# A blocked triangular solve that keeps its probabilities unscaled and puts the row's reciprocal into the row step

## The chip, the cores and the metric

The kernel runs on one core of a Trainium2 chip. The metric is the device time of one execution in microseconds (us). Engines are named as in the profile: PE (matrix engine; PEld is its weight load), DVE (vector engine), ACT (scalar engine), POOL (GpSimd) and SP (the queue that issues most DMAs).

## What is computed

Two layers on an input of 8 x 512 x 128 floats. The change lies in the attention of the second layer; its last lines decide:

```python
probs = jax.nn.softmax(logits + causal_mask, axis=-1)
L = jnp.eye(s) - jnp.tril(probs, -1)
rhs = jnp.diagonal(probs, axis1=-2, axis2=-1)[..., None] * v
A = jax.scipy.linalg.solve_triangular(L, rhs, lower=True)
return A.transpose(0, 2, 1, 3).reshape(b, s, HID) @ Wd.T + bd
```

For each of 8 x 16 = 128 pairs of batch and head, with head width 8 and 512 positions, row t of A is `p[t,t] * v[t]` plus the sum over all earlier rows k of `p[t,k] * A[k]`. Here p is a softmax: an exponential E divided by the row's sum Z.

## The kernel before

The 128 pairs of batch and head lie on the 128 partitions. The 512 positions are taken in four blocks I of 128. For each block `attend` makes the exponentials (tile `Ed` holds those of the block's own square), and sums up, over all keys of earlier blocks, `E * A` and the row sum Z; both lie in `RT`. Then `solve_block` solves the block itself, in four quarters c of 32 positions. The feed-forward experts of the layer (`ExpertSteps`, 10 tiles in each block, 2, 2, 3 and 3 of them in the four quarters) run in the same stretch on PE, ACT and POOL.

One quarter of `solve_block` goes as follows.

- PE turns the quarter's exponentials (`turn_probs`, L1179, 16 transposes for half a quarter) into a bank. DVE multiplies them out of the bank by `rZ = 1/Z` into `Pn` (L1293). They are then probabilities.
- DVE turns what earlier blocks add (`turn_before`, L1285), takes the reciprocal (L1286), multiplies the sums by `rZ` into `term` (L1279) and adds that to `A` (L1282, in `add_term`).
- POOL multiplies `A` (so far v) by the diagonal of `Pn` (L1263) and then sets the diagonal to 1 (L1266).
- From the second quarter on, DVE also copies the rows of the quarter before, turned by PE (`turn_rows`, L1218), into `Apos` (`keep_rows`, L1301; ACT copies the other half at L1254). PE makes 128 small products of them with `Ed` (`later_sums`, L1228; each stands in the trace as two matmuls, 256 in all); DVE turns the result (L1305), multiplies by `rZ` and adds it (`add_later`).
- DVE runs the row steps: for r = 1 to 31, two multiplies (L1323, four of the eight head columns each, 4(r+1) elements) and two sums over k (L1329). Every step waits for the step before by the semaphore `row_done`: 124 instructions in a quarter.

Queues around it, in program order. PE, in quarter c: turns of quarter c+1, the expert tiles of quarter c, `turn_rows(c)`, `later_sums(c+1)`. ACT: for each expert tile a copy (L775), two GELUs (L782) and a copy (L789), then its half of the rows (L1254). POOL: L1263, L1266, then for each expert tile a copy of indices (L796) and two scattered DMAs (L800). DVE has no work of the experts here.

Of the kernel before, what the change touches and what calls it, by code (L numbers as in the profile page):

```python
# [12 lines left out]
P = 128  # L13
# [7 lines left out]
HD = D // NH  # L21
BH = B * NH
CAP = 1280
SUB = 32
# [893 lines left out]
def solve_attention(nc, A, Apos, Ed, rows_dram, o_dram, send_rest, w, k_stack, q_stack, vT_dram, max_dram):  # L918
# [10 lines left out]
    with ExitStack() as ctx:  # L929
# [15 lines left out]
        rZ = sb("rZ", [P, P])  # L945
        before = sb("before", [P, SUB, SUB])
        prod = sb("prod", [P, HD, SUB])
        later, term = sb("later", [P, SUB, SUB]), sb("later_term", [P, SUB, HD])
        mx = sb("mx", [P, 2, BH])
        mxp = sb("mxp", [P, 3, BH], BF16)  # L950
        mxT = sb("mxT", [P, 3, P], BF16)
# [23 lines left out]
        for I in range(-1, LT):  # L975
            attend(nc, I, A, vT_dram, ident, Kst, Qmax, Qexp, k_stack, q_stack, max_dram, mx, mxp, mxT,
                   masks, identb, Ed, Eoff, Apos, one, RT, bank, big, send_rest)
            if I >= 0:
                solve_block(nc, I, Ed, RT, before, rZ, Pn, prod, later, term, A, Apos, ident, bank, big[3], steps)


def attend(nc, I, A, vT_dram, ident, Kst, Qmax, Qexp, k_stack, q_stack, max_dram, mx, mxp, mxT, masks,
# [197 lines left out]
    return last  # L1180


def solve_block(nc, I, Ed, RT, before, rZ, Pn, prod, later, term, A, Apos, ident, bank, wide, steps):

    k0 = I * steps.N // LT
    tiles = [range(k0 + sum(TILES[:c]), k0 + sum(TILES[:c + 1])) for c in range(NSUB)]
# [3 lines left out]
    with ExitStack() as ctx:  # L1190
# [16 lines left out]
        @block.tensor  # L1207
        def _(pe):
            def turn_next(c):
                for g in range(per_sub * c, per_sub * (c + 1)):  # L1210
                    if g >= 2:
                        pe.wait_ge(probs_in, g - 1)
                    turn_probs(nc, Ed, ident, bank[g % 2], g).then_inc(probs_turned, 1)

            def turn_rows(c):
                pe.wait_ge(row_done, ops * (c + 1))
                for d in range(HD):
                    last = nc.tensor.transpose(wide[0:(c + 1) * SUB, d * P:(d + 1) * P], A[:, d, t0:t0 + (c + 1) * SUB], ident[:, :])  # L1218
                    if d % 4 == 3:
                        last.then_inc(rows_turned, 1)  # L1220

            def later_sums(c):
                pe.wait_ge(act_kept, c)
                pe.wait_ge(dve_kept, c)
                for t in range(SUB):
                    for g in range(4):
                        row = (I * BH + 4 * t + g) * (HD + 1)
                        last = nc.tensor.matmul(wide[SUB * g:SUB * (g + 1), t * SUB:(t + 1) * SUB], Apos[0:c * SUB, row:row + SUB],  # L1228
                                                Ed[0:c * SUB, SUB * g + t, c * SUB:(c + 1) * SUB], start=True, stop=True,
                                                skip_group_check=True)  # L1230
                last.then_inc(later_mm, 1)

            turn_probs(nc, Ed, ident, bank[1], 1).then_inc(probs_turned, 1)
            for c in range(NSUB):
                if c + 1 < NSUB:
                    turn_next(c + 1)
                for k in tiles[c]:
                    steps.turn(pe, k)
                    steps.up(pe, k)
                    steps.down(pe, k)  # L1240
                turn_rows(c)
                if c + 1 < NSUB:
                    later_sums(c + 1)

        @block.scalar
        def _(act):
            for c in range(NSUB):
                for k in tiles[c]:
                    steps.keep_turned(act, k)
                    steps.gelu(act, k)  # L1250
                    steps.keep_out(act, k)
# [3 lines left out]

        @block.gpsimd
        def _(pool):
            for c in range(NSUB):
                ts = slice(t0 + c * SUB, t0 + (c + 1) * SUB)
                first = c * SUB * SUB  # L1260
                diag = Pn.rearrange("p q k -> p (q k)")[:, first:first + (SUB - 1) * (SUB + 1) + 1:SUB + 1]
# [2 lines left out]
                                        ALU.mult).then_inc(own_done, 1)  # L1264
                pool.wait_ge(own_done, 2 * c + 1)
                nc.gpsimd.memset(diag, 1.0).then_inc(own_done, 1)  # L1266
                for k in tiles[c]:
                    steps.send(pool, k)
            if I == LT - 1:
# [3 lines left out]
        def _(dve):  # L1273
            base = Chain(dve, base_done)

            def add_term(c, sums):
                qs = slice(c * SUB, (c + 1) * SUB)
                ts = slice(t0 + c * SUB, t0 + (c + 1) * SUB)
                base(nc.vector.tensor_tensor(term[:, :, :], sums[:, :, 0:HD],  # L1279
                                             rZ[:, qs].rearrange("p (q a) -> p q a", a=1).broadcast_to([P, SUB, HD]), ALU.mult))  # L1280
                dve.wait_ge(own_done, 2 * c + 1)
                base(nc.vector.tensor_tensor(A[:, :, ts], A[:, :, ts], term[:, :, :].rearrange("p q d -> p d q"), ALU.add))  # L1282

            def turn_before(c):
                base(nc.vector.transpose(before[:, :, :], RT[:, c, :, :].rearrange("p t q -> p q t")))  # L1285
                base(nc.vector.reciprocal(rZ[:, c * SUB:(c + 1) * SUB], before[:, :, HD]))  # L1286

            def add_before(c):
                for g in range(per_sub * c, per_sub * (c + 1)):
                    gs = slice(g * TURN, (g + 1) * TURN)  # L1290
                    if g:
                        dve.wait_ge(probs_turned, g)
                    nc.vector.tensor_tensor(Pn[:, gs, :], bank[g % 2][:, 0:TURN * SUB].rearrange("p (q k) -> p q k", k=SUB),  # L1293
                                            rZ[:, gs].rearrange("p (q a) -> p q a", a=1).broadcast_to([P, TURN, SUB]),
                                            ALU.mult).then_inc(probs_in, 1)
                add_term(c, before)

            def keep_rows(c):
                ks = slice(c * SUB, (c + 1) * SUB)
# [2 lines left out]

            def add_later(c):
                dve.wait_ge(later_mm, c)
                base(nc.vector.transpose(later[:, :, :], wide[:, :].rearrange("p (t q) -> p q t", q=SUB)))  # L1305
                add_term(c, later)

            for c in range(NSUB):
                turn_before(c)
                if c:  # L1310
                    keep_rows(c - 1)
                add_before(c)
                if c:
                    add_later(c)
                dve.wait_ge(own_done, 2 * c + 2)
                k0 = t0 + c * SUB
                for r in range(1, SUB):
                    n = ops * c + 4 * (r - 1)
                    for i in range(2):
                        if r > 1:  # L1320
                            dve.wait_ge(row_done, n - 1 + i)
                        ds = slice(i * HD // 2, (i + 1) * HD // 2)
                        nc.vector.tensor_tensor(prod[:, ds, 0:r + 1], A[:, ds, k0:k0 + r + 1],  # L1323
                                                Pn[:, c * SUB + r:c * SUB + r + 1, 0:r + 1].broadcast_to([P, HD // 2, r + 1]),
                                                ALU.mult).then_inc(row_done, 1)
                    for i in range(2):
                        dve.wait_ge(row_done, n + 1 + i)
                        ds = slice(i * HD // 2, (i + 1) * HD // 2)
                        nc.vector.tensor_reduce(A[:, ds, k0 + r], prod[:, ds, 0:r + 1], AX_X, ALU.add).then_inc(row_done, 1)  # L1329
            keep_rows(NSUB - 1)  # L1330


# [308 lines left out]
```

## Time and profile before

| | us |
|---|---|
| median of 3 runs | 1409.95 (1408.22 to 1410.42) |
| the profiled execution | 1409.06 |
| its span, first to last instruction | 1407.1 |
| PE busy in it | 979.8 (70%) |
| DVE busy | 910.4 (65%) |
| ACT busy | 466.4 (33%) |
| POOL busy | 342.9 (24%) |
| mean granted TensorE clock | 0.821 |

The profile is of one execution, and all rows below are of that one. "x992" is a count; in the list of groups the number behind the bar is busy time in us, then the mean length of one instruction in ns, then idle time of the engine before such instructions and who ended it. In a timeline each row is one instruction, or a run of like ones without idle time between them: start, length of the run, engine, line, operation, tiles, count, and in brackets the idle time before it with who ended it. A granted clock of 1.00 is 2.4 GHz, 0.50 is 1.2 GHz. "issue" means that the engine waited for nothing that the profile shows.

### The profile page before, as it was taken

The numbers are of one execution on the slowest core, as the hardware profiler recorded it, in microseconds if no ns is written. First come the engines' busy times: TensorE is split into PE (matmuls) and PEld (weight loads), VectorE is DVE, ScalarE is ACT, GpSimd is POOL, SyncE is SP. The second block draws the span as 40 slices with busy tenths as digits, with TensorE's granted clock in tenths as the row PEclk, the third lists the DMA queues.
The fourth block names the chain that finished last, engine by engine and source line by source line (L and its number), as shares of the span: only waits on it lengthen the run. The fifth ranks groups of instructions, "written<-read, shape, count | busy, mean of one in ns | idle before, by whom it ended". The sixth has DMA issues, their size and how long they took to land. (4 is left out here: it accounts for less than half of the span.)

```text
span 1407.1 us, 29569 instructions
## 1 busy us (share of the span) xinstructions
PE 979.8 (70%) x10741; PEld 766.5 (54%) x10762; DVE 910.4 (65%) x3559; ACT 466.4 (33%) x1066; POOL 342.9 (24%) x390
## 2 busy tenths in 40 slices
PE   5376599970665057876769967769986768986754
PEld 5265499960621034665646556646665656765643
DVE  5666272216789065788858889858878970068767
ACT  1233244424224003311235411235522227931115
POOL 1277155540047170021210021210001220012221
PEclk9998799995579587966889966889977888986777
DMA  9397598836018864410044220044411005420008
GB/s 225 40 212 206 145 250 241 230 96 179 25 50 238 244 149 123 111 28 18 25 97 129 73 61 20 21 110 126 116 44 32 26 22 163 137 57 23 25 22 234
DMA packets 241824, 153.95 MB, mean 109 GB/s; under 512 B 80432, under 2 KB 226096, under 8 KB 241424
## 3 DMA queue, kind: packets, MB, share of 16 engines
q1 hardware_dynamic: 232528, 133.04, 37.1%
q0 software_dynamic: 9152, 19.02, 4.1%
q8 instruction: 86, 1.41, 0.4%
q14 instruction: 58, 0.48, 0.1%
HBM read 96.76 MB, written 55.24 MB: 108 GB/s over the span
## 5 line engine op out<-in xcount | busy, mean ns | idle before, releaser
L1157 DVE TENSOR_REDUCE mx<-banks 128x1 f32<-128x384 f32 (+3 forms) x352 | 203.1, 635 | 74.0 <-PE banks L1088 58.9
L1323 DVE TENSOR_TENSOR prod<-A,Kst_Pn 128x8 f32<-128x8 f32 (+30 forms) x992 | 179.5, 221 | 0.5
L1329 DVE TENSOR_REDUCE A<-prod 128x4 f32<-128x8 f32 (+30 forms) x992 | 174.8, 217 | 0.0
L800 POOL DMA_INDIRECT o_dram<-step_o,step_to x80 | 81.9, 1024 | 308.5 <-ACT step_o L789 296.3
L1137 ACT ACTIVATE Eoff<-banks 128x256 f32<-128x256 f32 (+2 forms) x192 | 114.9, 599 | 102.6 <-PE banks L1073 93.5
L1071 PE MATMUL banks<-Qexp,Kst_Pn 128*128 128x256 bf16 x640 | 115.4, 282 | 47.5 <-DMA Qmax<-q_stack 37.8
L1139 ACT ACTIVATE Ed<-banks 128x256 f32<-128x256 f32 x256 | 97.9, 382 | 111.5 <-PE banks L1073 111.5
L1084 PE MATMUL banks<-masks,identb 128*128 128x128 bf16 (+2 forms) x352 | 89.2, 254 | 61.0 <-DMA Qmax<-q_stack 51.1
L756 PE MATMUL banks<-step_xT,step_w 128*128 128x256 f32 x320 | 106.3, 490 | 22.5 <-issue 22.0
L1263 POOL TENSOR_TENSOR A<-A,Kst_Pn 128x256 f32<-128x256 f32 x16 | 15.8, 987 | 411.6 <-DVE Kst_Pn L1293 411.6
L1088 PE MATMUL banks<-Kst_Pn,Qmax 128*128 128x128 bf16 (+3 forms) x491 | 115.7, 306 | 0.0
L767 PE MATMUL banks<-step_w,step_h 128*128 128x128 f32 x640 | 94.1, 307 | 28.3 <-ACT step_h L782 28.3
L767 PEld LDWEIGHTS banks<-step_w,step_h 128*128 128x128 f32 x640 | 85.8, 216 | 48.7 <-ACT step_h L782 48.7
L1071 PEld LDWEIGHTS banks<-Qexp,Kst_Pn 128*128 128x128 bf16 x640 | 56.3, 100 | 84.0 <-DMA Qmax<-q_stack 38.9
L756 PEld LDWEIGHTS banks<-step_xT,step_w 128*128 128x128 f32 x320 | 74.7, 245 | 46.1 <-issue 33.8
L596 POOL DMA_INDIRECT o_dram<-e_o,e_to x78 | 76.2, 977 | 92.7 <-DVE e_o L617 80.5
L1179 PE MATMUL banks<-ident_c,Ed 32*128 32x32 f32 x512 | 78.5, 325 | 16.3 <-PEq L83 10.4
L587 ACT ACTIVATE e_h<-banks,e_b 128x256 f32<-128x256 f32 x156 | 63.2, 471 | 80.0 <-PE banks L557 80.0
L1179 PEld LDWEIGHTS banks<-ident_c,Ed 32*128 32x128 f32 x512 | 75.9, 254 | 19.0 <-issue 13.1
L1160 DVE COPY RT<-banks 128x512 f32<-128x512 f32 x32 | 22.1, 691 | 90.9 <-PE banks L1102 90.9
L557 PE MATMUL banks<-e_xT,e_w 128*128 128x256 f32 x312 | 76.2, 388 | 5.7 <-DMA e_b<-in_L_ffn_b_dram 5.0
L1084 PEld LDWEIGHTS banks<-masks,identb 128*128 128x128 bf16 x352 | 35.2, 100 | 80.6 <-DMA Qmax<-q_stack 52.9
(197 smaller groups left out, 1832.5 us busy)
## 6 DMA issues: line engine op xcount, KB each, us to landing
Kst_Pn<-k_stack SPq DMA_DIRECT2D x32, 512.0 KB, 4.1
rows_dram<-blank SPq DMA_DIRECT2D x12, 858.0 KB, 11.6
e_w<-in_L_w1T_dram SPq DMA_DIRECT2D x39, 256.0 KB
e_w<-in_L_w2T_dram SPq DMA_DIRECT2D x39, 256.0 KB
Qmax<-q_stack SPq DMA_DIRECT2D x64, 96.0 KB
Qexp<-q_stack SPq DMA_DIRECT2D x64, 96.0 KB
Kst_Pn<-k_stack SPq DMA_DIRECT2D x16, 384.0 KB, 4.3
step_xt<-rows_dram SPq DMA_DIRECT2D x40, 132.0 KB, 2.2
```

The costliest lines, as they stand in the source:

```text
L756: last = self.nc.tensor.matmul(self.up_banks[i][:, (hc % 2) * TS:(hc % 2 + 1) * TS], self.w1[e % 2][:, hc * P:(hc + 1) * P], self.xT[:, :] ...
L767: last = self.nc.tensor.matmul(self.down_bank[:, j * D:(j + 1) * D], self.h[:, hc, j * P:(j + 1) * P], self.w2[e % 2][:, hc, :], start=(hc ...
L800: self.nc.gpsimd.indirect_dma_start(self.o_dram, bass.IndirectOffsetOnAxis(self.to[n][:, j:j + 1], 0), self.o[n][:, j, :], None).then_inc( ...
L1071: last = nc.tensor.matmul(out, Kst[b % 2][:, s, J * P:(J + 1) * P], Qexp[b % 2][:, 2 * s:2 * s + 2, :], start=True, stop=(J < I), skip_gro ...
L1084: nc.tensor.matmul(diagonal, identb[:, :], masks[:, 0:1, :].broadcast_to([P, per_bank, P]), start=True, stop=False, skip_group_check=True)
L1088: last = nc.tensor.matmul(out[:, j * keys_ahead:(j + 1) * keys_ahead], Qmax[b % 2][:, h, :], Kst[b % 2][:, h // 2, 0:keys_ahead], start=Fa ...
L1137: nc.scalar.activation(Eoff[:, n % 4, 0:I, :, :].rearrange("p j h q -> p (j h q)"), big[n % n_big][:, 0:I * 2 * P], ACT.Exp, scale=scale)
L1139: nc.scalar.activation(Ed[:, :, :].rearrange("p (g t) q -> p g t q", g=4)[:, 2 * (n % 2):2 * (n % 2) + 2, n // 2, :], big[n % n_big][:, I ...
L1157: nc.vector.tensor_reduce(out, logits, AX_X, ALU.max, negate=True).then_inc(max_done, 1)
L1179: last = nc.tensor.transpose(out[:, i * SUB:(i + 1) * SUB], Ed[ks, :, g * TURN + i], ident[ks, ks])
L1323: nc.vector.tensor_tensor(prod[:, ds, 0:r + 1], A[:, ds, k0:k0 + r + 1], Pn[:, c * SUB + r:c * SUB + r + 1, 0:r + 1].broadcast_to([P, HD / ...
L1329: nc.vector.tensor_reduce(A[:, ds, k0 + r], prod[:, ds, 0:r + 1], AX_X, ALU.add).then_inc(row_done, 1)
```

## The change

- `Pn` holds exponentials that aren't divided by Z. ACT copies them out of the bank (`keep_probs`), where DVE multiplied them; for quarter c+1 it does so ahead of the expert tiles of quarter c.
- The sums of earlier blocks and of earlier quarters are added to `A` unscaled, straight from the turned tile; the multiplies by `rZ` into `term` are gone.
- The division is done in the row step: the two multiplies become `scalar_tensor_tensor` with `rZ[:, row]`, one value for each partition, as the scalar. Row 0 of a quarter, which had no step, gets one multiply of 128x8.
- In `later_sums` the two sides are exchanged: `Ed` is loaded as weights and 8 columns of `Apos` stream, where 32 columns of `Apos` were the weights and 32 of `Ed` streamed. The result takes 256 columns of the bank and not 1024, so DVE turns 128x256.
- POOL's `own(c+1)` (L1263, L1266) goes ahead of the sends of quarter c. DVE turns what earlier blocks add to quarter c+1 right behind `keep_rows(c-1)`, and in the first quarter ahead of the row steps; the reciprocal and the add stand ahead of `keep_rows`.

```diff
             def turn_rows(c):
-                pe.wait_ge(row_done, ops * (c + 1))
+                pe.wait_ge(row_done, (ops + 1) * (c + 1))
...
-                        last = nc.tensor.matmul(wide[SUB * g:SUB * (g + 1), t * SUB:(t + 1) * SUB], Apos[0:c * SUB, row:row + SUB],
-                                                Ed[0:c * SUB, SUB * g + t, c * SUB:(c + 1) * SUB], start=True, stop=True,
-                                                skip_group_check=True)
+                        last = nc.tensor.matmul(wide[SUB * g:SUB * (g + 1), t * HD:(t + 1) * HD],
+                                                Ed[0:c * SUB, SUB * g + t, c * SUB:(c + 1) * SUB], Apos[0:c * SUB, row:row + HD],
+                                                start=True, stop=True, skip_group_check=True)
...
         def _(act):
+            def keep_probs(c):
+                for g in range(per_sub * c, per_sub * (c + 1)):
+                    if g:
+                        act.wait_ge(probs_turned, g)
+                    nc.scalar.copy(Pn[:, g * TURN:(g + 1) * TURN, :],
+                                   bank[g % 2][:, 0:TURN * SUB].rearrange("p (q k) -> p q k", k=SUB)).then_inc(probs_in, 1)
+
+            keep_probs(0)
             for c in range(NSUB):
+                if c + 1 < NSUB:
+                    keep_probs(c + 1)
                 for k in tiles[c]:
...
         def _(pool):
-            for c in range(NSUB):
+            def own(c):
...
+            own(0)
+            for c in range(NSUB):
+                if c + 1 < NSUB:
+                    own(c + 1)
                 for k in tiles[c]:
                     steps.send(pool, k)
...
-            def add_term(c, sums):
-                qs = slice(c * SUB, (c + 1) * SUB)
+            def add_sums(c, sums):
                 ts = slice(t0 + c * SUB, t0 + (c + 1) * SUB)
-                base(nc.vector.tensor_tensor(term[:, :, :], sums[:, :, 0:HD],
-                                             rZ[:, qs].rearrange("p (q a) -> p q a", a=1).broadcast_to([P, SUB, HD]), ALU.mult))
-                dve.wait_ge(own_done, 2 * c + 1)
-                base(nc.vector.tensor_tensor(A[:, :, ts], A[:, :, ts], term[:, :, :].rearrange("p q d -> p d q"), ALU.add))
+                base(nc.vector.tensor_tensor(A[:, :, ts], A[:, :, ts], sums, ALU.add))
...
+            def add_before(c):
                 base(nc.vector.reciprocal(rZ[:, c * SUB:(c + 1) * SUB], before[:, :, HD]))
...
+                dve.wait_ge(own_done, 2 * c + 2)
+                add_sums(c, before[:, :, 0:HD].rearrange("p q d -> p d q"))
...
-                base(nc.vector.transpose(later[:, :, :], wide[:, :].rearrange("p (t q) -> p q t", q=SUB)))
-                add_term(c, later)
-
+                base(nc.vector.transpose(later[:, :, :], wide[:, 0:SUB * HD].rearrange("p (t d) -> p d t", d=HD)))
+                add_sums(c, later[:, :, :])
+
+            turn_before(0)
             for c in range(NSUB):
-                turn_before(c)
+                add_before(c)
                 if c:
                     keep_rows(c - 1)
-                add_before(c)
+                if c + 1 < NSUB:
+                    turn_before(c + 1)
                 if c:
                     add_later(c)
-                dve.wait_ge(own_done, 2 * c + 2)
-                k0 = t0 + c * SUB
+                k0, q0 = t0 + c * SUB, c * SUB
+                n = (ops + 1) * c + 1
+                nc.vector.tensor_tensor(A[:, :, k0], A[:, :, k0], rZ[:, q0:q0 + 1].broadcast_to([P, HD]), ALU.mult).then_inc(row_done, 1)
+                dve.wait_ge(row_done, n)
                 for r in range(1, SUB):
-                    n = ops * c + 4 * (r - 1)
                     for i in range(2):
...
-                        nc.vector.tensor_tensor(prod[:, ds, 0:r + 1], A[:, ds, k0:k0 + r + 1],
-                                                Pn[:, c * SUB + r:c * SUB + r + 1, 0:r + 1].broadcast_to([P, HD // 2, r + 1]),
-                                                ALU.mult).then_inc(row_done, 1)
+                        nc.vector.scalar_tensor_tensor(out=prod[:, ds, 0:r + 1], in0=A[:, ds, k0:k0 + r + 1], scalar=rZ[:, q0 + r:q0 + r + 1],
+                                                       in1=Pn[:, q0 + r:q0 + r + 1, 0:r + 1].broadcast_to([P, HD // 2, r + 1]),
+                                                       op0=ALU.mult, op1=ALU.mult).then_inc(row_done, 1)
```

## Rows read from the trace of the kernel before

**Rows 1.** The costliest groups of instructions on the page: the multiplies of the row steps

```profile
L1323 DVE TENSOR_TENSOR prod<-A,Kst_Pn 128x8 f32<-128x8 f32 (+30 forms) x992 | 179.5, 221 | 0.5
```

**Rows 2.** Timeline of DVE: the head of the third block, up to its second row step

```profile
1042.78 2.53 DVE L1285 STREAM_TRANSPOSE before<-RT 128x1024 f32<-128x1024 f32 x1 [2.66 <-PEq L83]
...
1048.26 0.70 DVE L1282 TENSOR_TENSOR A<-A,later_term 128x256 f32<-128x256 f32 x1 [0.91 <-POOL A L1263]
1048.99 0.24 DVE L1323 TENSOR_TENSOR prod<-A,Kst_Pn 128x8 f32<-128x8 f32 x2
...
1049.39 0.25 DVE L1323 TENSOR_TENSOR prod<-A,Kst_Pn 128x12 f32<-128x12 f32 x2
```

**Rows 3.** Timeline of DVE: from the end of quarter 0 to the rows of quarter 1

```profile
1065.74 0.48 DVE L1323 TENSOR_TENSOR prod<-A,Kst_Pn 128x128 f32<-128x128 f32 x2
1066.14 0.47 DVE L1329 TENSOR_REDUCE A<-prod 128x4 f32<-128x128 f32 x2
1066.53 1.94 DVE L1285 STREAM_TRANSPOSE before<-RT 128x1024 f32<-128x1024 f32 x1
...
1068.89 1.04 DVE L1301 COPY Apos<-banks 32x512 f32<-32x512 f32 x1
...
1075.80 1.25 DVE L1305 STREAM_TRANSPOSE later<-banks 128x1024 f32<-128x1024 f32 x1 [2.98 <-PE banks L1228]
...
1077.55 0.69 DVE L1282 TENSOR_TENSOR A<-A,later_term 128x256 f32<-128x256 f32 x1
1078.27 0.24 DVE L1323 TENSOR_TENSOR prod<-A,Kst_Pn 128x8 f32<-128x8 f32 x2
```

**Rows 4.** Timeline of DVE in the first layer: instructions with a scalar per partition, back to back

```profile
325.01 1.14 DVE L669 SCALAR_TENSOR_TENSOR c_r<-c_r,wt 128x128 f32<-128x128 f32 x4 [17.20 <-ACT c_r L691]
327.72 0.88 DVE L669 SCALAR_TENSOR_TENSOR c_r<-c_r,wt 128x128 f32<-128x128 f32 x3 [1.57 <-ACT c_r L691]
...
74.68 1.13 DVE L357 SCALAR_TENSOR_TENSOR s<-banks,rq,xr 128x128 f32<-128x128 f32 x4 [1.95 <-PE banks L272]
```

**Rows 5.** Timeline of POOL: its multiply in the third block, a copy near the end

```profile
1047.11 1.04 POOL L1263 TENSOR_TENSOR A<-A,Kst_Pn 128x256 f32<-128x256 f32 x1 [120.28 <-DVE Kst_Pn L1293]
...
1377.39 0.62 POOL L1372 COPY rows_b<-Apos 128x512 f32<-128x512 f32 x1 [1.77 <-PE banks L1393]
```

**Rows 6.** Timeline of DVE in the stretch of that copy

```profile
1376.90 1.51 DVE L1432 SCALAR_TENSOR_TENSOR last_r<-last_r,wt 128x128 f32<-128x128 f32 x4 [14.24 <-ACT last_r L1412]
```

**Rows 7.** Groups of instructions by line: ACT copies of a bank into SBUF

```profile
L182 ACT COPY xnT<-banks 128x512 f32<-128x512 f32 x8 | 4.7, 587 | 15.7 <-PE banks L165 15.7
```

**Rows 8.** Timeline of PE in the third block: turns, and the small products

```profile
1042.78 2.50 PE L1179 MATMUL banks<-ident_c,Ed 32*128 32x32 f32 x16 [3.13 <-PEq L83]
...
1070.08 1.99 PE L1228 MATMUL banks<-Ed,Apos 32*32 32x32 f32 x130 [2.37 <-DVE Apos L1301]
1073.75 1.93 PE L1228 MATMUL banks<-Ed,Apos 32*32 32x32 f32 x126 [1.69 <-issue]
...
1102.93 1.50 PE L1228 MATMUL banks<-Ed,Apos 64*32 64x32 f32 x94 [1.72 <-issue]
...
1127.75 1.04 PE L1218 MATMUL banks<-ident_c,A 128*96 128x128 f32 x8
1130.10 1.67 PE L1228 MATMUL banks<-Ed,Apos 96*32 96x32 f32 x167 [1.31 <-DVE Apos L1301]
```

**Rows 9.** Windows of PE: stretch, length, busy time (count), granted clock, DMA share, GB/s

```profile
1066.66:1067.70 1.04, 1.04 (x8) 1.00 0.19 63
1070.10:1075.70 5.60, 3.91 (x257) 0.50 0.03 6
1130.10:1135.20 5.10, 2.87 (x257) 0.93 0.11 32
1298.50:1300.41 1.91, 1.91 (x8) 0.50 0.20 69
```

**Rows 10.** Timeline of DVE: the wait at the end of quarter 2

```profile
1128.89 1.05 DVE L1301 COPY Apos<-banks 32x512 f32<-32x512 f32 x1 [2.03 <-PE banks L1218]
```

More of the change, by code:

```diff
@@ L947, in solve_attention @@
         prod = sb("prod", [P, HD, SUB])
-        later, term = sb("later", [P, SUB, SUB]), sb("later_term", [P, SUB, HD])
+        later = sb("later", [P, HD, SUB])
         mx = sb("mx", [P, 2, BH])
@@ L978, in solve_attention @@
             if I >= 0:
-                solve_block(nc, I, Ed, RT, before, rZ, Pn, prod, later, term, A, Apos, ident, bank, big[3], steps)
+                solve_block(nc, I, Ed, RT, before, rZ, Pn, prod, later, A, Apos, ident, bank, big[3], steps)
 def attend(nc, I, A, vT_dram, ident, Kst, Qmax, Qexp, k_stack, q_stack, max_dram, mx, mxp, mxT, masks,
@@ L1180, in turn_probs, with solve_block @@
     return last
-def solve_block(nc, I, Ed, RT, before, rZ, Pn, prod, later, term, A, Apos, ident, bank, wide, steps):
+def solve_block(nc, I, Ed, RT, before, rZ, Pn, prod, later, A, Apos, ident, bank, wide, steps):
     k0 = I * steps.N // LT
@@ L1274, in _ @@
             base = Chain(dve, base_done)
-            def add_term(c, sums):
-                qs = slice(c * SUB, (c + 1) * SUB)
+            def add_sums(c, sums):
                 ts = slice(t0 + c * SUB, t0 + (c + 1) * SUB)
-                base(nc.vector.tensor_tensor(term[:, :, :], sums[:, :, 0:HD],
-                                             rZ[:, qs].rearrange("p (q a) -> p q a", a=1).broadcast_to([P, SUB, HD]), ALU.mult))
-                dve.wait_ge(own_done, 2 * c + 1)
-                base(nc.vector.tensor_tensor(A[:, :, ts], A[:, :, ts], term[:, :, :].rearrange("p q d -> p d q"), ALU.add))
+                base(nc.vector.tensor_tensor(A[:, :, ts], A[:, :, ts], sums, ALU.add))
             def turn_before(c):
                 base(nc.vector.transpose(before[:, :, :], RT[:, c, :, :].rearrange("p t q -> p q t")))
+            def add_before(c):
                 base(nc.vector.reciprocal(rZ[:, c * SUB:(c + 1) * SUB], before[:, :, HD]))
[L1288 to L1296, printed above, removed]
+                dve.wait_ge(own_done, 2 * c + 2)
+                add_sums(c, before[:, :, 0:HD].rearrange("p q d -> p d q"))
             def keep_rows(c):
@@ L1329, in _ @@
                         nc.vector.tensor_reduce(A[:, ds, k0 + r], prod[:, ds, 0:r + 1], AX_X, ALU.add).then_inc(row_done, 1)
+                    n += 4
             keep_rows(NSUB - 1)
```

## Prediction

> **What bounds the kernel now.** I read the page first: the row steps of the solver are among its costliest groups, 992 multiplies with almost no idle time ahead of them [rows 1]. Then I read DVE's timeline through one block. In the third block quarter 0 starts its rows at 1048.99 [rows 2] and ends them at 1066.14 + 0.47 = 1066.61 [rows 3], so the row phase takes 17.62 us, and DVE doesn't pause in it. Sixteen such phases make 282 us of the span. Between two row phases lies a chain over three engines: PE turns the rows, DVE and ACT copy them (DVE from 1068.89), PE makes the small products from 1070.08, DVE waits 2.98 for them, turns, multiplies, adds, and the rows of quarter 1 start at 1078.27 [rows 3, 8]. That is 11.66 us. The reader should see that the multiplies by 1/Z which DVE does meanwhile lie in front of a wait for PE: they are no part of this chain, and taking them away only makes the wait longer. What counts is DVE's row phase, and behind it the chain of turn, copy, products and add. One quarter differs. At the end of quarter 2 DVE waits 2.03 for PE's turned rows [rows 10], and PE had no wait ahead of that turn [rows 8]: three expert tiles hold PE longer than the rows hold DVE. So a slower row phase costs time in quarters 0, 1 and 3 of each block, and in quarter 2 only beyond that wait.
>
> **The change part by part**, for one block; there are four.
>
> *Row steps.* Each quarter has 62 multiplies, and all of them become multiplies with a scalar per partition. The two multiplies of 128 elements in the last row start 0.40 before the sum behind them, 0.20 each [rows 3]. Four `scalar_tensor_tensor` of 128 elements, back to back, take 1.14 together and three take 0.88; that gives 0.26 from start to start [rows 4]. So the scalar costs 0.06 us per instruction, and since these starts follow each other without a wait, nothing hides it. 62 x 0.06 = 3.8 us. In the shortest rows the chain already waits: the first row takes 1049.39 - 1048.99 = 0.40 [rows 2], about 0.07 more than four issues of such length, and some ten rows have a falling part of that; this absorbs about 0.3. I take 3.5 us for a quarter, with 3.0 and 3.8 as ends. An end at nothing, or below, would need the scalar's fetch to lie under the instruction ahead; the rows speak against it, and it is a rival below. On the path it counts three times: +10.5 us.
>
> Here two rules of the Trainium skill can be held against the rows. The page "VectorE: DVE Perf Modes" (section "The TRN2 errata — SBUF-src ops pay a fixed extra latency per instruction") gives a vector instruction from SBUF to SBUF a fixed 58 cycles plus its elements, and names no term for a scalar operand; by that, an estimate from its figures, both kinds of multiply take 0.19 us at 128 elements and the row step costs nothing. Its figure fits the plain multiply (0.20) and not the one with a scalar (0.26), so the measured row decides. The page "Vector Engine (DVE) Microarchitecture Reference" (section 7, "Points that are easy to get wrong") says that a `scalar_tensor_tensor` with two SBUF sources that aren't bf16 runs at half throughput. In this trace it doesn't: four of them with both sources in SBUF take 1.14, and four with one source in PSUM take 1.13 [rows 4].
>
> *Small products.* The count stays, 256 matmuls, and so does the stall in the middle of them, in which PE waits for nothing that the profile shows ("issue", 1.69 and 1.72 here [rows 8]); I take it for a wait for PE's own instructions. At a granted clock of 0.50 130 matmuls take 1.99, 0.0153 each; at 0.93 167 take 1.67, 0.0100 each [rows 8, 9]. With 8 columns to stream and not 32 I take 0.0100 at the low clock too. The part ahead of the stall is bound to the arrival of instructions, so only the 126 behind it gain: 126 x 0.005 = 0.6. At the high clock I count 0.2. For the three rounds of a block: -1.1 us, with 0 and -2.0 as ends.
>
> *From the products to the rows.* Now 1078.27 - (1073.75 + 1.93) = 2.59. After it: a wait of 0.1, a turn of 256 columns in place of 1024 (between 1.25 / 4 = 0.31 and 0.5, I take 0.45), an add of 0.65, row 0's multiply of 0.2 with its wait, and gaps between them: 1.5. This gains 1.05 in quarters 1 and 3: -2.1 us. In quarter 2 it falls into the wait for PE.
>
> *From the rows to the products.* Now DVE's turn and reciprocal stand ahead of its copy, and products start 1070.08 - 1066.61 = 3.47 behind the rows [rows 3, 8]. Afterwards a reciprocal and an add (1.0 us) stand there and PE's turn decides: 1.04 at a granted clock of 1.00, 1.91 at 0.50 [rows 9]. With 0.15 for two semaphores and 1.19 from the copy's start to the products, that gives 2.4 or 3.25. Both levels stand in this trace ahead of like work. PE finishes its tiles first and will then sit idle for the rest of a row phase that is longer than now, so I take the low clock: -0.3 in quarters 0 and 1, -0.6 us in all; at the high clock it is -2.1. At the end of quarter 3 the same turn may come at the low clock too, +0.8; I count half, +0.4.
>
> *The head.* Now 6.21 from the block's start to the first row [rows 2]. After it, ACT's copy of the second half (0.59 [rows 7]) follows PE's 16 turns of 2.50 [rows 8], then POOL's multiply of 1.04 [rows 5] and its memset: DVE gets to its add at about 4.5, adds until 5.3, turns quarter 1's sums for 1.94 ahead of the rows, and does row 0's multiply: 7.4. +1.2 us. The turn moved here was not on the chain in quarter 1 except ahead of the copy, which is counted above.
>
> *POOL's multiply inside the row phase.* Now DVE waits for it between phases. After it, `own(c+1)` runs as soon as ACT has copied, during the rows of quarter c. A POOL copy of 0.62 that reads SBUF stretched four `scalar_tensor_tensor` from 1.14 to 1.51 [rows 4 to 6], 0.37 lost. POOL's multiply takes 0.96 to 1.04, so about 0.6 is lost in each of quarters 0 and 1: +1.2 us (ends 0 and 1.9). In quarter 2 it is covered by the wait for PE.
>
> *ACT's copies.* 8 x 0.59 in a block. The second one of each quarter starts when PE goes on to turn the first tile, and ACT's copy of that tile queues behind it, and PE behind that: between 0 and 0.6, I take 0.45. In quarter 2, where PE decides, that is +0.45 us (the upper end is 2, should PE's clock rise one tile later). Elsewhere it hides under the rows. That quarter has room for the rest: products end at 1102.93 + 1.50 = 1104.43, the copy starts at 1128.89, so PE's way takes 24.46 [rows 8, 10]; DVE's takes 1.5 + 17.62 + 3.5 + 0.6 + 1.0 = 24.2. If that cover were gone, each further 0.1 us would count.
>
> Sum for a block: 10.5 - 1.1 - 2.1 - 0.6 + 0.4 + 1.2 + 1.2 + 0.45 = +9.95. Four blocks: +39.8. The profiled execution took 1409.06 (0.89 under the median of the three runs), so the forecast is 1409.06 + 39.8 = 1449 us. The multiplies that leave DVE (Pn, term) give nothing beyond this, since they lay before waits for POOL or PE.
>
> **The rivals.**
>
> *The chain's shortening is worth more.* PE keeps the high clock at the turns (-2.1 in place of -0.6), the products gain 2.0, the clock costs nothing at the end, POOL's multiply fits between, and a row phase costs 3.2: 9.6 - 2.0 - 2.1 - 2.1 + 1.2 + 0.45 = +5.05 a block, 1429 us. Against it speaks the longer idle time of PE ahead of each turn. 0.14.
>
> *The scalar is free.* This is the side of a gain: if its fetch lies under the instruction ahead, the row phase stays at 17.62, and the shortened chain remains, 1.2 + 1.2 - 1.1 - 2.1 - 0.6 + 0.45 = -0.95 a block, 1405 us; without POOL's collision 1400. It decides once the scalar costs a multiply under 0.95 / (3 x 62) = 0.005 us. For it: these instructions wait on semaphores, those in [rows 4] don't. Against it: these waits are nearly all over by the time of issue in the long rows. Its chance is 0.08. By the cost table of the Trainium skill's page "VectorE: DVE Perf Modes", named above, this rival would hold.
>
> *Two SBUF sources halve the rate.* A multiply streams 0.001 us per element, 68 elements on average, so a quarter would lose 62 x 0.068 = 4.2 more, and quarter 2 would lose its cover: +4.2 x 3 + 4.3 = 17 a block more, 1517 us. The rows show no such thing [rows 4]. 0.02.
>
> *The change doesn't do what it says* in one part: the exchanged products stay bound to the arrival of instructions. That is the end of 0 above, +4.4 us: 1453, inside the forecast.
>
> **How the numbers follow.** The forecast case, 1432 to 1466, has 0.76; with the first rival at 0.14, the free scalar at 0.08 and the halved rate at 0.02. The range of 8 in 10 goes from 1422 to 1466. A difference under 0.2% (2.8 us) can't be told from no change here. Slower by more than that takes the forecast and both slower rivals, 0.92 less 0.03 for what I don't see: 0.89. Faster has 0.08, same 0.03.
>
> **What the profile will show.** Right: the multiplies of the row step about 0.06 longer and a row phase of about 21 us; a turn of 128x256 of about 0.45; DVE's copy behind the rows about 2 us after them; one stretched row step in quarters 0 and 1; quarter 2 unchanged in length from products to copy. The forecast is wrong if the row phase stays under 18.5, if quarter 2 gets longer by more than 1 us, or if the head gets shorter.

## The result and the profile after

| | before | after |
|---|---|---|
| median (us) | 1410.18 (1408.22 to 1412.49) | 1444.14 (1442.37 to 1445.11) |
| ratio after / before | | 1.0232, 95% interval 1.0213 to 1.0251 |
| the profiled execution | 1409.06 | 1443.83 |
| its span | 1407.1 | 1441.8 |

The change makes the kernel 2.3% slower: 34.8 us between the two profiled executions, where +39.8 was forecast. The row steps, in the list of groups of after (columns as in [rows 1]):

```profile
L1331 DVE SCALAR_TENSOR_TENSOR prod<-A,rZ,Kst_Pn 128x8 f32<-128x8 f32 (+30 forms) x992 | 246.2, 289 | 0.6
```

Against [rows 1] the same 992 multiplies are busy 66.7 us longer (246.2 - 179.5). The timeline of DVE in the third block of after shows the head and the first row steps (these answer to [rows 2]), and then the way from quarter 0 to quarter 1 (to [rows 3]):

```profile
1064.38 2.52 DVE L1296 STREAM_TRANSPOSE before<-RT 128x1024 f32<-128x1024 f32 x1 [2.91 <-PEq L83]
...
1068.85 0.60 DVE L1293 TENSOR_TENSOR A<-A,before 128x256 f32<-128x256 f32 x1 [1.57 <-POOL Kst_Pn L1276]
1069.49 1.92 DVE L1296 STREAM_TRANSPOSE before<-RT 128x1024 f32<-128x1024 f32 x1
1071.44 0.17 DVE L1324 TENSOR_TENSOR A<-A,rZ 128x8 f32<-128x8 f32 x1
1071.65 1.03 DVE L1331 SCALAR_TENSOR_TENSOR prod<-A,rZ,Kst_Pn 128x8 f32<-128x8 f32 x2
...
1092.44 0.60 DVE L1331 SCALAR_TENSOR_TENSOR prod<-A,rZ,Kst_Pn 128x128 f32<-128x128 f32 x2
1092.97 0.47 DVE L1337 TENSOR_REDUCE A<-prod 128x4 f32<-128x128 f32 x2
...
1095.48 1.05 DVE L1306 COPY Apos<-banks 32x512 f32<-32x512 f32 x1 [1.16 <-PE banks L1218]
...
1102.56 0.45 DVE L1310 STREAM_TRANSPOSE later<-banks 128x256 f32<-128x256 f32 x1 [4.28 <-PE banks L1228]
1103.05 0.42 DVE L1293 TENSOR_TENSOR A<-A,later 128x256 f32<-128x256 f32 x1
...
1103.71 0.36 DVE L1331 SCALAR_TENSOR_TENSOR prod<-A,rZ,Kst_Pn 128x8 f32<-128x8 f32 x2
```

The two multiplies of 128 elements start 1092.97 - 1092.44 = 0.53 ahead of the sum behind them, 0.265 each, where it was 0.20. The row phase runs from 1071.65 to 1093.44, 21.8 us where it was 17.6. The head takes 7.27 (1064.38 to 1071.65). The first pair of multiplies takes 1.03 in quarter 0 and 0.36 in quarter 1, and POOL's timeline of after has the reason:

```profile
1071.66 0.85 POOL L1273 TENSOR_TENSOR A<-A,Kst_Pn 128x256 f32<-128x256 f32 x1 [2.92 <-ACT Kst_Pn L1251]
```

POOL's multiply of the next quarter starts 0.01 after that pair and ends at 1072.51; the pair ends at 1072.68. PE in the same block of after, first in its timeline (this answers to [rows 8]), then in windows (columns as in [rows 9]):

```profile
1093.49 1.89 PE L1218 MATMUL banks<-ident_c,A 128*32 128x128 f32 x8 [7.42 <-DVE A L1337]
1096.67 1.95 PE L1228 MATMUL banks<-Apos,Ed 32*32 32x8 f32 x130 [1.30 <-DVE Apos L1306]
1100.55 1.88 PE L1228 MATMUL banks<-Apos,Ed 32*32 32x8 f32 x126 [1.92 <-issue]
```

```profile
1093.50:1095.50 2.00, 1.88 (x8) 0.50 0.00 0
1096.67:1102.43 5.76, 3.83 (x257) 0.50 0.02 6
1125.45:1126.60 1.15, 1.05 (x8) 1.00 0.17 57
1158.74:1163.50 4.76, 2.76 (x257) 0.92 0.11 34
```

PE waits 7.42 for the rows of quarter 0, and its turn of them runs at a granted clock of 0.50; behind quarter 1 the turn (1125.45) runs at 1.00. The products take as long as before although 8 columns stream and not 32.

Now the end of the third block, which the rows ahead of the prediction don't show. The timelines of DVE, POOL and SP, first of before, then of after:

```profile
1156.56 1.06 DVE L1301 COPY Apos<-banks 32x512 f32<-32x512 f32 x1 [1.21 <-PE banks L1218]
...
1157.67 0.97 POOL L800 DMA_INDIRECT o_dram<-step_o,step_to  x1 [0.31 <-issue]
...
1161.47 0.33 SPq L1031 DMA_DIRECT2D Kst_Pn<-k_stack  x1
```

```profile
1185.38 0.47 DVE L1337 TENSOR_REDUCE A<-prod 128x4 f32<-128x128 f32 x2
...
1187.23 1.06 DVE L1306 COPY Apos<-banks 32x512 f32<-32x512 f32 x1 [1.39 <-PE banks L1218]
...
1186.34 0.96 POOL L800 DMA_INDIRECT o_dram<-step_o,step_to  x1 [0.30 <-issue]
...
1190.15 0.33 SPq L1031 DMA_DIRECT2D Kst_Pn<-k_stack  x1
```

In both kernels the next stage's first load stands at the same distance behind POOL's last send of the block: 1161.47 - 1158.64 = 2.83 and 1190.15 - 1187.30 = 2.85. The distance to DVE's last copy isn't the same: 3.85 and 1.86. The same holds in blocks 0 and 1: 2.84 behind the last send in both kernels, 3.84 behind the copy in before, 1.78 and 1.55 in after. Where the copy does end a block, in the run after_tiles below, the load stands closer, 0.75 behind it (timelines of DVE and SP, third block):

```profile
1186.83 1.06 DVE L1310 COPY Apos<-banks 32x512 f32<-32x512 f32 x1 [2.06 <-PE banks L1218]
...
1188.64 0.33 SPq L1031 DMA_DIRECT2D Kst_Pn<-k_stack  x1
```

So the scattered DMAs of the last expert tile end the block, before and after; DVE's rows don't.

### The profile page after: what moved, and what is told of

The parts are those of the page before. It is cut to its first block and busy times, and to the rows that moved or that the text cites. A ratio compares the mean times of both kernels' runs of the same rounds, so it can differ in the third digit from the quotient of the medians.

```text
span 1441.8 us, 29546 instructions
## 1 busy us (share of the span) xinstructions
PE 1003.8 (70%) x10762; PEld 784.2 (54%) x10762; DVE 932.7 (65%) x3515; ACT 485.9 (34%) x1098; POOL 333.6 (23%) x390
## 5 line engine op out<-in xcount | busy, mean ns | idle before, releaser
L1331 DVE SCALAR_TENSOR_TENSOR prod<-A,rZ,Kst_Pn 128x8 f32<-128x8 f32 (+30 forms) x992 | 246.2, 289 | 0.6
L1337 DVE TENSOR_REDUCE A<-prod 128x4 f32<-128x8 f32 (+30 forms) x992 | 178.5, 217 | 0.0
L767 PE MATMUL banks<-step_w,step_h 128*128 128x128 f32 x640 | 104.5, 330 | 27.8 <-ACT step_h L782 27.8
L1088 PE MATMUL banks<-Kst_Pn,Qmax 128*128 128x128 bf16 (+3 forms) x512 | 122.3, 310 | 0.0
L767 PEld LDWEIGHTS banks<-step_w,step_h 128*128 128x128 f32 x640 | 95.6, 236 | 48.4 <-ACT step_h L782 48.4
L756 PE MATMUL banks<-step_xT,step_w 128*128 128x256 f32 x320 | 106.5, 491 | 21.7 <-issue 21.1
L1179 PE MATMUL banks<-ident_c,Ed 32*128 32x32 f32 x512 | 75.6, 325 | 12.2 <-PEq L83 10.8
```

The lines of the kernel that those rows point to most:

```text
L756: last = self.nc.tensor.matmul(self.up_banks[i][:, (hc % 2) * TS:(hc % 2 + 1) * TS], self.w1[e % 2][:, hc * P:(hc + 1) * P], self.xT[:, :] ...
L767: last = self.nc.tensor.matmul(self.down_bank[:, j * D:(j + 1) * D], self.h[:, hc, j * P:(j + 1) * P], self.w2[e % 2][:, hc, :], start=(hc ...
L1088: last = nc.tensor.matmul(out[:, j * keys_ahead:(j + 1) * keys_ahead], Qmax[b % 2][:, h, :], Kst[b % 2][:, h // 2, 0:keys_ahead], start=Fa ...
L1179: last = nc.tensor.transpose(out[:, i * SUB:(i + 1) * SUB], Ed[ks, :, g * TURN + i], ident[ks, ks])
L1331: nc.vector.scalar_tensor_tensor(out=prod[:, ds, 0:r + 1], in0=A[:, ds, k0:k0 + r + 1], scalar=rZ[:, q0 + r:q0 + r + 1], in1=Pn[:, q0 + r: ...
```

## The experiments

My theory after the result: each multiply pays for fetching its scalar, this reaches the end only in quarters 0 and 1, and the expert tiles set the length of quarters 2 and 3. The rivals: it is the form with two operations that is slow, not the scalar; and the exchanged products lose what they should gain.

| run | median | before beside it | ratio (95%) |
|---|---|---|---|
| imm_scalar | 1408.47 | 1407.95 | 0.9998 (0.9978 to 1.0018) |
| pool_between | 1450.02 | 1407.95 | 1.0302 (1.0261 to 1.0342) |
| sides_only | 1405.44 | 1407.95 | 0.9985 (0.9962 to 1.0008) |
| narrow_weights | 1406.14 | 1407.95 | 0.9992 (0.9968 to 1.0016) |
| order_only | 1400.40 | 1409.44 | 0.9939 (0.9921 to 0.9957) |
| sides_order | 1401.34 | 1409.44 | 0.9922 (0.9891 to 0.9952) |
| sides_order_tiles | 1373.88 | 1409.44 | 0.9755 (0.9738 to 0.9773) |
| after_tiles | 1438.94 | 1409.44 | 1.0203 (1.0182 to 1.0224) |
| before_tiles | 1391.74 | 1406.91 | 0.9889 (0.9852 to 0.9926) |
| order_tiles | 1385.32 | 1406.91 | 0.9852 (0.9819 to 0.9885) |

**imm_scalar**: the kernel after, with an immediate as the scalar. It leaves out the division of rows 1 to 31 of each quarter.

```diff
-  nc.vector.scalar_tensor_tensor(..., scalar=rZ[:, q0 + r:q0 + r + 1],
+  nc.vector.scalar_tensor_tensor(..., scalar=1.0,
```

> The changed kernel with the constant 1.0 as the scalar of the row step's multiplies, in place of the row's 1/Z from SBUF; it leaves out the division of rows 1 to 31 of each quarter. Theory: the fetch of a scalar per partition is the whole cost of the new multiply. Then two multiplies of 128 elements start 0.20 us apart again (0.26 in the changed kernel), the row phase is 18.2 us in quarters 0 to 2 and 17.6 in quarter 3 (21.7 and 21.1), and the time falls to about 1409: 2 x 3.5 us a block in quarters 0 and 1, nothing in quarter 2, where PE's tiles take as long, and some 1.7 in quarter 3, where the scattered DMAs of the last tile then set the end of the block. Rival: the form with two operations costs it, whatever the scalar. Then the row phase stays at 21.7 and the time at 1444.

Group and timeline of DVE in the third block of imm_scalar:

```profile
L1331 DVE SCALAR_TENSOR_TENSOR prod<-A,Kst_Pn 128x8 f32<-128x8 f32 (+30 forms) x992 | 187.0, 229 | 0.5
```

```profile
1055.38 0.93 DVE L1331 SCALAR_TENSOR_TENSOR prod<-A,Kst_Pn 128x8 f32<-128x8 f32 x2
...
1072.77 0.48 DVE L1331 SCALAR_TENSOR_TENSOR prod<-A,Kst_Pn 128x128 f32<-128x128 f32 x2
1073.17 0.47 DVE L1337 TENSOR_REDUCE A<-prod 128x4 f32<-128x128 f32 x2
```

Measured: 0.20 for each of the two last multiplies again (1073.17 - 1072.77 = 0.40), row phases of 17.61 to 17.64 in the fourth quarters and 18.05 to 18.33 where POOL's multiply lies inside, and a time that can't be told from before. The operation, its two sources in SBUF and its two arithmetic steps are those of after; only the column of scalars is gone. So the column as a scalar is what costs 0.06 us, 992 times. The eight row phases of quarters 0 and 1 are 28.0 us shorter here than in after, together. The profiled execution is 35.3 us shorter: in this run the products, and the way to them in quarters 0 and 1, also take about 5 us less in all; the rest isn't followed.

**pool_between**: the kernel after, with POOL's multiply held back until the rows of the quarter are done.

```diff
-                if c + 1 < NSUB:
-                    own(c + 1)
                 for k in tiles[c]:
                     steps.send(pool, k)
+                if c + 1 < NSUB:
+                    pool.wait_ge(row_done, (ops + 1) * (c + 1))
+                    own(c + 1)
```

> The changed kernel, but POOL's multiply and memset for the next quarter wait until the rows of this one are done, behind the sends. Theory: in the changed kernel POOL's multiply holds DVE up by 0.55 us in the row phases of quarters 0 to 2 (21.7 there, 21.1 in quarter 3). Then all sixteen row phases take 21.1. DVE waits for POOL behind the rows instead, its copy of the rows comes at about 2.0 and not 1.3 to 1.8 us after them, so the time hardly moves: 1440 to 1446. Rival: the 0.55 comes from something else that runs in these phases (PE, ACT). Then they stay at 21.7, and the time rises by 2 to 6 us.

Timelines of DVE and of POOL in pool_between, at the end of quarter 2:

```profile
1159.34 0.34 DVE L1300 RECIPROCAL rZ<-before 128x32 f32<-128x32 f32 x1
1164.74 0.59 DVE L1294 TENSOR_TENSOR A<-A,before 128x256 f32<-128x256 f32 x1 [5.05 <-POOL Kst_Pn L1276]
```

```profile
1162.57 0.97 POOL L800 DMA_INDIRECT o_dram<-step_o,step_to  x1 [0.30 <-issue]
1163.57 0.86 POOL L1273 TENSOR_TENSOR A<-A,Kst_Pn 128x256 f32<-128x256 f32 x1
```

Measured: all sixteen row phases take 21.05 to 21.12, so the collision costs 0.55 to 0.7 us in a phase of 21.7. The kernel got slower all the same, by more than I had expected: POOL's multiply now stands behind the sends of the third tile, and DVE waits 5.05 for it in quarter 2. The early place on POOL costs less than this late one.

On the collision the Trainium skill's page "SBUF — State Buffer" (section "Who interferes with whom") says that a vector instruction with two SBUF inputs contends with a GpSimd instruction that reads SBUF. The rows of after agree: the pair that takes 0.36 undisturbed takes 1.03 beside a POOL multiply of 0.85.

**sides_only** and **narrow_weights**: before, with the exchanged products alone (8 columns stream, the result in 256 columns, turned by 128x256); and before, with only 8 of 32 weight columns loaded.

```diff
-  matmul(wide[.., t * SUB:(t + 1) * SUB], Apos[0:c * SUB, row:row + SUB], Ed[...])
+  matmul(wide[.., t * HD:(t + 1) * HD], Ed[...], Apos[0:c * SUB, row:row + HD])      # sides_only
+  matmul(wide[SUB * g:SUB * g + HD, ..], Apos[0:c * SUB, row:row + HD], Ed[...])     # narrow_weights
```

> The kernel before with one part of the change alone: the small products with exchanged sides, and DVE's turn of 256 columns. Theory from the trace after: the products themselves take as long as before (3.6 us without stalls at a granted clock of 0.50, 2.5 at 0.92), whatever streams; the gain lies in the turn (1.25 to 0.45) and the add (0.65 to 0.43) behind them, 2.59 to about 1.6 us from products to rows. On the path that is -1.0 us in quarter 1 of each block, nothing in quarter 2 (PE's tiles) and little in quarter 3 (tiles and sends set the end there): 1402 to 1408. Rival, the step of the forecast: the products get 0.6 us shorter at the low clock too, 1398 to 1402.

> The kernel before, but the small products load only the 8 columns of weights that are used, in place of 32; 32 columns stream as before. If the load of weights sets their pace at the low clock, the products without stalls fall from 3.6 us at a granted clock of 0.50 to 3.0 or less, and the time by 1 to 4 us. If it is a floor for each instruction, 3.6 stays and the time stays within 1408 to 1412. With the runs of 8 streamed columns this tells which of the two sides counts, if any.

Timeline and window of PE in narrow_weights, the first products of the third block:

```profile
1065.01 1.97 PE L1228 MATMUL banks<-Ed,Apos 32*8 32x32 f32 x130 [2.37 <-DVE Apos L1301]
```

```profile
1065.00:1066.50 1.50, 1.49 (x115) 0.50 0.04 11
```

Measured: 130 matmuls in 1.97 with 8 weight columns, 1.95 in after with 8 streamed columns, 1.99 in before [rows 8]. So in this stretch the pace, 0.015 us for each at a granted clock of 0.50, follows neither side's columns. Neither kernel can be told from before; narrow_weights lies just under the 1408 to 1412 that I had expected, with before at 1407.95 beside it. In sides_only the way from products to rows is 1.0 shorter (1.51 to 1.54 in most rounds, 2.50 to 2.59 before), and quarter 1 of each block gets that much shorter; the 4 us that this would give lie within the interval of the ratio, and the time doesn't show them.

**order_only** and **sides_order**: before with DVE's copy ahead of its turn, without and with the exchanged products.

```diff
             for c in range(NSUB):
-                turn_before(c)
                 if c:
                     keep_rows(c - 1)
+                turn_before(c)
                 add_before(c)
```

> The kernel before, with DVE's order alone changed: the copy of the turned rows stands ahead of the turn of the sums, which the changed kernel does too in its own way. Theory: in quarters 0 and 1 the copy then starts at 1.2 us behind the rows (PE's turn at a granted clock of 1.00) or 2.0 (0.50), against 2.28 before, and products start that much sooner; quarters 2 and 3 are set by PE's tiles and gain nothing. DVE's 2.3 us of turn and reciprocal go into its wait for the products. That is 0.3 to 1.1 us in each of eight quarters: 1400 to 1406 where the kernel before takes 1408. Rival: the moved work (2.3 us) and POOL's multiply behind it become the late ones, products end first, and the time stays within 1406 to 1411.

> The kernel before with the exchanged products and with that order, so the changed kernel's shorter chain without unscaled probabilities, without the scalar in the row step and without POOL's multiply inside the rows. Theory: products to rows 1.55 for 2.56, rows to products 0.3 to 1.1 us sooner, row phases 17.62. In quarter 1 both gains meet PE's tiles, which end about 1 us ahead of the rows before, so part of them is lost: -1.5 to -3 us a block, 1396 to 1403. It should beat the changed kernel by 40 us or more. Rival: PE's tiles take up all of it from quarter 1 on, 1403 to 1408.

Measured: with the order alone, products start 2.33 to 3.18 behind the rows in quarters 0 and 1, in four of the eight at 2.3 to 2.4 (3.44 to 3.48 before), and the time falls by 9 us. The exchange adds nothing to it that can be told from the spread: 1401.3 and 1400.4, with one of the seven runs of sides_order at 1387.95. Why it doesn't is seen in the lengths of quarters 2 and 3, below.

**sides_order_tiles**: sides_order, and in PE's and ACT's queues the turn of the next expert tile goes ahead of the second product of the present one. **after_tiles**, **before_tiles** and **order_tiles** are the kernel after, before and order_only with the same edit.

```diff
+                steps.turn(pe, tiles[c][0])
                 for k in tiles[c]:
-                    steps.turn(pe, k)
                     steps.up(pe, k)
+                    if k + 1 in tiles[c]:
+                        steps.turn(pe, k + 1)
                     steps.down(pe, k)
...
+                steps.keep_turned(act, tiles[c][0])
                 for k in tiles[c]:
-                    steps.keep_turned(act, k)
                     steps.gelu(act, k)
+                    if k + 1 in tiles[c]:
+                        steps.keep_turned(act, k + 1)
                     steps.keep_out(act, k)
```

> The same, and in each quarter PE turns the next expert tile, and ACT copies it, ahead of the tile's last products, so that ACT's copy (0.62 us of waiting before each further tile) is hidden. Theory: in this kernel PE's tiles set the ends of quarters 2 and 3, so 1.2 us less of PE's way in each shows in the time: 2 to 2.4 us a block less than the run without it, about 1389 to 1395. Rival: the ends are set by DVE's rows, then it gains under 0.5 us a block.

> The changed kernel with the same reordering of the expert tiles. Theory: with rows of 21.7 us DVE sets the end of quarters 0, 1 and 3 and ties with PE in quarter 2, so PE's shorter way gains only in quarter 2 of the blocks where PE was late by up to 2 us, and the block's end doesn't move: 0 to -6 us in all, 1438 to 1445. Rival: the changed kernel still waits for PE's tiles in quarters 2 and 3, then it gains 8 us or more, as in the kernel without the scalar.

> The kernel before with the reordering of the expert tiles alone. Theory: quarters 2 and 3 of the kernel before are set by PE's tiles, and the reordering shortens a tile behind the first by 1.07 us (5.54 to 4.47 in the run with all three parts) and the first one by about 1 us of clock; so the wait at the end of quarter 2 and the time from the last row to the next block shrink as they did there, 20 to 28 us in all: 1381 to 1389. Rival: it needs the shorter chain of the other two parts to show; then it gains under 12 us.

> The kernel before with DVE's order and the reordering of the tiles, without the exchanged products. Theory: with PE's tiles out of the way the 1.0 us that the exchange saves between products and rows lies on the path in quarters 1 to 3 of each block, so this run is 6 to 12 us slower than the run with all three parts (1374): 1380 to 1386. Rival: the exchange still gains nothing, as it did with the old order of the tiles; 1373 to 1377.

Timeline of PE in quarter 2 of the third block, of sides_order and then of sides_order_tiles:

```profile
1108.97 3.78 PE L767 MATMUL banks<-step_w,step_h 128*128 128x128 f32 x16 [0.69 <-ACT step_h L782]
1112.54 0.63 PE L745 MATMUL banks<-ident_c,step_xt 128*128 128x128 f32 x2
...
1116.34 2.05 PE L767 MATMUL banks<-step_w,step_h 128*128 128x128 f32 x16 [0.69 <-ACT step_h L782]
...
1121.88 2.05 PE L767 MATMUL banks<-step_w,step_h 128*128 128x128 f32 x16 [0.69 <-ACT step_h L782]
```

```profile
1097.02 2.67 PE L767 MATMUL banks<-step_w,step_h 128*128 128x128 f32 x16 [0.26 <-ACT step_h L782]
...
1101.25 0.38 PE L745 MATMUL banks<-ident_c,step_xt 128*128 128x128 f32 x2
1102.10 2.05 PE L767 MATMUL banks<-step_w,step_h 128*128 128x128 f32 x16 [0.47 <-ACT step_h L782]
...
1106.57 2.05 PE L767 MATMUL banks<-step_w,step_h 128*128 128x128 f32 x16 [0.69 <-ACT step_h L782]
```

A tile's period falls from 1121.88 - 1116.34 = 5.54 to 1106.57 - 1102.10 = 4.47, since the turn and its copy now lie under the GELUs; and the first tile's second product takes 2.67 and not 3.78. sides_order_tiles is faster than both kernels by far, and gained more over sides_order (27 us) than I had expected (8 to 10). after_tiles gained only 5 over after, within what I had expected. before_tiles gained 15, short of the 20 to 28 expected and above the 12 of the rival; its quarter 2 takes 22.5 in all four blocks, its quarter 3 from 23.2 to 24.1. order_tiles came out 11 us above sides_order_tiles, as expected. The first two follow from one table, the length in us from the end of the products to DVE's copy (quarter 2, blocks 0 to 3) and to the next stage (quarter 3, blocks 0 to 2), read from the timelines:

| kernel | quarter 2 | quarter 3 |
|---|---|---|
| before | 24.07, 24.44, 24.47, 26.28 | 26.26, 26.22, 26.30 |
| after | 26.31, 24.19, 24.18, 26.31 | 26.35, 26.28, 26.61 |
| imm_scalar | 24.04, 26.28, 26.24, 24.49 | 26.35, 26.21, 24.80 |
| sides_only | 24.00, 26.27, 26.15, 26.30 | 23.94, 26.26, 24.54 |
| sides_order | 26.20, 24.38, 26.21, 24.39 | 24.13, 26.34, 26.37 |
| after_tiles | 24.20, 24.19, 24.19, 24.20 | 26.20, 26.19, 26.18 |
| sides_order_tiles | 22.24, 22.19, 22.88, 22.14 | 23.06, 23.66, 22.84 |

In the first five rows the lengths lie between 23.9 and 24.8 or between 26.1 and 26.6, though a row phase takes 17.6 us in three of these kernels, 17.6 to 18.3 in imm_scalar and over 21 in after: the chain of three expert tiles sets them. The two of 24.2 in after are a tie: PE's turn starts right behind the tiles, without idle time, and 0.05 and 0.09 us behind DVE's last row. In the third block of after, the timelines of DVE and PE:

```profile
1155.84 0.47 DVE L1337 TENSOR_REDUCE A<-prod 128x4 f32<-128x128 f32 x2
...
1156.40 1.04 PE L1218 MATMUL banks<-ident_c,A 128*96 128x128 f32 x8
```

With the new order of the tiles the ends follow DVE where it is slow: in after_tiles both columns are constant (1.3 + 21.7 + 1.2 = 24.2 in quarter 2), and there the next stage's first load stands 0.75 behind DVE's last copy and over 6 us behind POOL's last send in blocks 0 to 2. So the slow rows of after use up what the tile order would give, and the exchanged products can be seen in the time only once the tiles are out of the way: order_tiles stands at 0.9852 of before, sides_order_tiles at 0.9755.

## Why the prediction was right in its size, and where it was not

The third block took 118.70 before and 125.78 after, +7.1 where the sum said +9.95. By its terms:

| part of the third block | forecast | measured |
|---|---|---|
| the scalar in the row steps, quarters 0 and 1 | +7.0 | +6.9 |
| POOL's multiply in them | +1.2 | +1.3 |
| the products, three rounds | -1.1 | +0.4 |
| products to rows, quarter 1 | -1.05 | -1.3 |
| rows to products, quarters 0 and 1 | -0.6 | -1.3 |
| the head | +1.2 | +1.1 |
| quarter 2, from products to DVE's copy | +0.45 | -0.3 |
| quarter 3, from products to the next stage | +2.85 | +0.3 |
| sum | +9.95 | +7.1 |

*The row step* was right in mechanism and size. A phase without a POOL multiply takes 21.11 where it took 17.66: +3.45, with 3.5 forecast from [rows 4]. imm_scalar shows that it is the scalar. With it falls the free-scalar rival, but its sum was near: it said 1405 us, or 1400, and imm_scalar, where the scalar is free, takes 1408.5. By the cost table of the Trainium skill's page "VectorE: DVE Perf Modes" (section "The TRN2 errata — SBUF-src ops pay a fixed extra latency per instruction"), 58 cycles plus the elements, both multiplies would take the same, an estimate from its figures. The measured step is 0.265 with the scalar and 0.20 without, and the measurement decides. The rival of two SBUF sources is out by the same run: both sources lie in SBUF there, and the pace is that of the plain multiply.

*Quarter 3* is the step that failed. The prediction had it that a slower row phase costs time "in quarters 0, 1 and 3", and gave this quarter 3.5 - 1.05 + 0.4 = 2.85. I had looked at who ends quarter 2 and had found the expert tiles [rows 10], but hadn't asked the same question at the end of the block, where three tiles run too. There the last send of POOL decides, before and after, and the rows grow under its cover: the quarter changes by +0.09, +0.06 and +0.31 in blocks 0 to 2, where the sum had +2.85.

*The small products* failed in the other direction. The step from 32 to 8 columns was to bring 0.0153 down to 0.0100 at the low clock. It didn't: 1.88 / 126 = 0.0149. I had read two points at two clocks ([rows 8, 9]) as a cost of streaming; at the low clock the cost stands for each instruction, whatever streams. The forecast's end of "0" held; that the arrival of instructions causes it, as the prediction had it, no run shows. The stalls stayed as they were (27.5 us in 15 of them in after, 25.6 in 14 before).

*From rows to products* the forecast took the low clock at the turns of both quarters. It is there in all four quarters 0 of after (products 3.24 behind the rows), but only in one of four quarters 1 (3.08; the others 2.42 to 2.43). The term itself was -0.44 by the prediction's own rows (3.47 - 3.25 = 0.22, twice), not -0.6.

*Quarter 2*: the tie of 24.46 against 24.2 held in blocks 1 and 2, where the quarter now takes 24.2 and tiles and rows end together. In block 0 the tiles took 26.31, 2.24 more than before: PE's clock rose one tile later, which the prediction had named as the upper end of this term. This, and a second stall in the products behind it (8.32 us for products that took 4.75), make block 0 the dearest, +12.3. A quarter 2 longer by more than 1 us was one of the prediction's signs of being wrong, and in this block it came true. Whether the change causes the later clock and the second stall isn't settled: sides_only, where ACT copies nothing more than before, has the long quarter 2 in three blocks, and before has it in block 3 (26.28) and products of 7.78 and 7.47 us in two other rounds.

So the forecast of 1449 came near the 1444.14 partly by luck: two misses had opposite signs, -2.55 a block from quarter 3 and +1.5 from the products. Over four blocks the differences are +12.3, +6.9, +7.1 and +5.6, together 31.8 of the 34.7 us of span. Without the surplus of block 0, whose cause is open, four blocks would come to some 26. Of the rest 1.9 us lie ahead of the first block, which starts at 597.87 in before and at 599.77 in after, and 1.0 between and behind the blocks.

## What to carry to other kernels

A scalar from a column of SBUF isn't free in a chain of short vector instructions: before a multiply is folded into such a chain, set its price in the chain against the place that the separate multiply has now. Here most of the multiplies by 1/Z lay before waits. Two places were on the way to the rows, as the timeline of DVE in the third block of before shows: the multiplies into `Pn` at the head, which POOL waits for, and the one behind the products, 0.42 us a round.

```profile
1045.73 1.29 DVE L1293 TENSOR_TENSOR Kst_Pn<-banks,rZ 128x512 f32<-128x512 f32 x2
...
1077.09 0.42 DVE L1279 TENSOR_TENSOR later_term<-later,rZ 128x256 f32<-128x256 f32 x1
```

For each stretch of a loop ask who ends it, and ask it again for each turn of the loop: here, before the change, two quarters of four belonged to the rows and two to the expert tiles, and an edit that can't be told from before alone (the exchanged sides) gave about 1% once the engine that covered it had been shortened.

## What the runs showed of the hardware that I had not expected

- A scalar from a column of SBUF costs a vector multiply 0.06 us (the mean over all 992 is 289 ns, with an immediate in its place 229), and a row phase 3.45 us.
- Small matmuls, one behind the other on groups of 32 output partitions, go at 0.015 us each at a granted clock of 0.50, for 8 or 32 streamed columns and for 8 or 32 loaded ones. What sets this floor the runs don't show.
- Each round of 256 such products holds a stall of 1.1 to 2.8 us, and a few hold two, in which PE waits for nothing that the profile names. The prediction took it for a wait for PE's own instructions; no run tests that.
- Three expert tiles take one of two lengths, about 2 us apart, in kernels that don't differ in them. The first tile's second product makes the difference, in the timelines of PE in quarter 2 of before (third block, the short form) and of after (first block, the long form):

```profile
1114.78 2.05 PE L767 MATMUL banks<-step_w,step_h 128*128 128x128 f32 x16 [0.69 <-ACT step_h L782]
```

```profile
680.16 3.78 PE L767 MATMUL banks<-step_w,step_h 128*128 128x128 f32 x16 [0.69 <-ACT step_h L782]
```

In sides_order, where this product takes 3.78 too, the window over it (1108.97 to 1112.54) has a granted clock of 0.50, and the one over the next tile's (2.05) has 1.00. What makes the clock rise ahead of it or behind it stays open.
